# Second operand of two leaky activations read from PSUM

## The reference

```python
def _leaky(x):
    return jnp.where(x >= 0, x, LEAKY_SLOPE * x)        # LEAKY_SLOPE = 0.01
...
gp = _leaky(jnp.einsum('th,ehm->etm', x, w_gate))       # 8 experts, m = 128
up = jnp.einsum('th,ehm->etm', x, w_up)
y_all = jnp.einsum('etm,emh->eth', gp * up, w_down)
...                                                     # the two chosen experts, weighted
p = _leaky(hidden_states @ sw_gate) * (hidden_states @ sw_up) @ sw_down   # shared, 256 wide
y = y + p
```

## Time and profile before

| | us |
|---|---|
| median of 3 executions | 2302.65 |
| the three executions | 2302.65, 2306.17, 2302.55 |
| the profiled execution | 2303.26 |
| its span, first to last instruction | 2301.5 |
| shared expert, first L2270 to last L2275 | 1193.8 to 1266.7 |
| tile mixture, first L2149 to last L2154 | 1277.9 to 1366.0 |

### The profile page before, as it was taken

The page is one execution under the profiler, slowest core; times in us unless marked ns, Lnnn a source line. Parts: engine busy times, 40 slices in busy tenths (PEclk is TensorE's granted clock), DMA queues, the critical chain, the costliest instruction groups (busy, mean ns, idle before and its releaser), DMA issues. The chain is left out here.

```text
span 2301.5 us, 44687 instructions
## 1 busy us (share of the span) xinstructions
PE 2009.0 (87%) x15891; PEld 1415.9 (62%) x15891; DVE 1115.0 (48%) x3338; ACT 990.1 (43%) x2602; POOL 585.4 (25%) x972
## 2 busy tenths in 40 slices
PE   6899999887999996899967775996879999969994
PEld 3477777654777775566644454883557777736662
DVE  5388882264888824200043346106568883331112
ACT  2388881155888811111113231223668883212221
POOL 2022210076111105211124243115821111421111
PEclk9999999898999998899978985998989999979997
DMA  2185523001643121433121532741010004131113
GB/s 84 51 241 153 149 63 96 0 1 43 166 112 105 44 74 44 145 103 103 54 95 55 161 116 87 238 140 41 1 50 21 21 12 148 45 121 47 46 44 118
DMA packets 156763, 197.80 MB, mean 86 GB/s; under 512 B 15187, under 2 KB 129838, under 8 KB 156556
## 3 DMA queue, kind: packets, MB, share of 16 engines
q1 hardware_dynamic: 144940, 168.83, 24.1%
q0 software_dynamic: 11616, 26.26, 3.2%
HBM read 120.33 MB, written 88.64 MB: 91 GB/s over the span
## 5 line engine op out<-in xcount | busy, mean ns | idle before, releaser
L990 ACT ACTIVATE att_pr<-all_h,att_nmax 128x128 f32<-128x128 f32 (+3 forms) x768 | 420.8, 551 | 50.7 <-DVE att_nmax L943 50.7
L1054 PEld LDWEIGHTS att_t_ps<-all_ident,att_pr 64*128 64x128 f32 x3840 | 163.1, 139 | 104.3 <-issue 48.7
L1054 PE MATMUL att_t_ps<-all_ident,att_pr 64*128 64x64 f32 x3840 | 170.0, 223 | 10.4 <-DVE att_pt L952 10.3
L1249 PE MATMUL out_y_ps<-outw_wo,mem_qt 128*128 128x256 f32 x768 | 178.5, 386 | 0.0
L1897 PE MATMUL exp_f_h_ps<-exp_f_xs_t,cw_f_w 128*128 128x512 f32 (+1 forms) x512 | 171.9, 495 | 1.5 <-DVE exp_f_xs_t L1934 1.5
L1909 PE MATMUL exp_f_y_ps<-cw_f_w,exp_f_hid 128*128 128x256 f32 x768 | 168.4, 379 | 0.0
L952 DVE COPY att_pt<-att_t_ps 128x1024 f32<-128x1024 f32 (+2 forms) x168 | 166.5, 991 | 0.0
L1249 PEld LDWEIGHTS out_y_ps<-outw_wo,mem_qt 128*128 128x128 f32 x768 | 144.3, 193 | 24.8 <-issue 6.2
L1964 ACT ACTIVATE exp_f_hid<-exp_f_h_ps 128x512 f32<-128x512 f32 (+1 forms) x128 | 62.5, 491 | 221.0 <-PE exp_f_h_ps L1897 218.1
L1909 PEld LDWEIGHTS exp_f_y_ps<-cw_f_w,exp_f_hid 128*128 128x128 f32 x768 | 144.8, 190 | 19.5 <-issue 0.5
L943 DVE CUSTOM_DVE_ANT_0 all_h<-att_s_ps,att_bias,mem1k_nsn 128x128 f32<-128x128 f32 (+3 forms) x256 | 128.3, 548 | 35.6 <-PE att_s_ps L1037 26.7
(11 more groups left out here) (390 smaller groups left out, 3712.4 us busy)
## 6 DMA issues: line engine op xcount, KB each, us to landing
sorted_c<-all_zero SPq DMA_DIRECT2D x8, 2056.0 KB, 13.8
sorted_f<-all_zero SPq DMA_DIRECT2D x8, 2056.0 KB, 11.9
cw_f_w<-in_L_ffn_w_dram SPq DMA_DIRECT2D x16, 1024.0 KB, 8.0
cw_f_w<-in_L_ffn_W_dram SPq DMA_DIRECT2D x16, 1024.0 KB, 8.1
com_f_rows<-expert_f SPq DMA_DIRECT2D x20, 512.0 KB, 6.7
band<-rev SPq DMA_DIRECT2D x2, 4096.0 KB, 19.4
att_bias<-band SPq DMA_DIRECT2D x32, 256.0 KB, 3.0
tw_f_wab<-in_L_ffn_w_dram SPq DMA_DIRECT2D x2, 4096.0 KB, 19.7
```

The lines of the kernel that those rows point to most:

```text
L990: nc.scalar.activation(pr[u % 4][:, hh, at], sc[u % 4][:, hh, at], ACT.Exp, scale=-1.0, bias=nmax[:, b + k, q, h:h + 1], accum_out=rsum[:, ...
L1054: last = nc.tensor.transpose(t_ps[e % 2][:, half, (q + 1) * (n * hh + k) + kb, :], pr[u % 4][d, hh, at:at + P], c.ident[d, d])
L1249: nc.tensor.matmul(y_ps[b % 2][:, q, :], c.out_t[:, p, P * at:P * (at + 1)], wo[:, p, :], start=(p == 0), stop=False)
```

## The change

In both places the leaky activation's second tensor operand (`in1`) becomes the gate half of the PSUM tile, in place of the SBUF copy that ScalarE made of it. The first operand stays that copy, so ScalarE's copy, its semaphore and VectorE's waits stay as they are. No instruction is added, removed or moved, and no wait is changed.

```diff
@@ experts_by_tile, block.vector
-                        nc.vector.scalar_tensor_tensor(out=lin[t % 2][:], in0=act[t % 2][:], scalar=0.01, in1=act[t % 2][:], op0=ALU.mult,
+                        nc.vector.scalar_tensor_tensor(out=lin[t % 2][:], in0=act[t % 2][:], scalar=0.01, in1=ab_ps[t % 2][:, 0, :], op0=ALU.mult,
                                                        op1=ALU.max).then_inc(lin_ready, 1)
@@ SharedExpert.vector
-            nc.vector.scalar_tensor_tensor(out=self.lin[n][:], in0=self.act[n][:], scalar=0.01, in1=self.act[n][:], op0=ALU.mult,
+            nc.vector.scalar_tensor_tensor(out=self.lin[n][:], in0=self.act[n][:], scalar=0.01, in1=self.gu_ps[n][:, 0, :], op0=ALU.mult,
                                            op1=ALU.max).then_inc(self.lin_ready, 1)
```

## The result

| | before | after |
|---|---|---|
| median, us | 2302.65 | 2316.55 |
| lowest and highest execution | 2300.18 to 2306.96 | 2313.43 to 2321.47 |
| profiled execution, us | 2303.26 | 2321.47 |
| its span, us | 2301.5 | 2319.7 |
| first to last L2270, us | 72.1 | 85.9 |

The medians are of five executions each, taken in one comparison. The ratio is 1.0067, with a 95% interval of 1.0050 to 1.0084. The forecast was no change, with a range of 2299.5 to 2306.3 us. It was wrong: the kernel is 13.9 us slower.

What follows compares the result with a forecast made beforehand. TensorE (87% of the span) was taken to bound the tile mixture; VectorE (48%) was not the bound on average. Path terms, none there and -0.015 us in the shared expert, added 0.0 to the 2302.65 us median: 2302.7, range 2299.5 to 2306.3.

Steps and rivals of the forecast that it cites:

- Length of the instructions: Both stages: changed instructions last as long as neighbours with one PSUM operand, L2149 287 ns and L2270 421 ns.
- The dear end: Both stages: upper bound from attention's custom instruction, 348 and 479 ns, 3.4 us in all if everything were on the path.
- What the spread can give back: Shared expert: L2270's excess over its shortest, if lost to a neighbour and gone after the change, returns at most 0.14 us.
- the change part by part: Both stages: order and waits stay, only 55 instructions' operand place changes; busy time -0.08 us (L2270) and +0.20 us (L2149).
- How much of it lies on the path: Tile mixture: none; shared expert: -0.015 us, or +0.16 us at the upper bound.
- 3 instructions of 16 count: Shared expert: TensorE waited for `shx_hid` in 3 of 16 tiles, so only those lengths matter, 3 x -5 ns.
- Rival 1: TensorE, after waits on `hid`: a few ns of shift add one 10 us low-clock stretch, 4.9 us, 2307.6 us; chance 0.04.
- Rivals 2 to 4: Both stages: all PSUM start-ups exposed, 2306.1 (chance 0.04); low-clock stretch avoided, 2299.2 or 2297.8 (0.04); operand still SBUF, 2302.65 (under 0.01).
- The tile mixture: L2149's edit puts nothing on the path, as VectorE waits 0.94 us for TensorE in each tile.
- the cover that the prediction counted on: Tile mixture: VectorE's 0.94 us wait, and 0.56 us in the last tile, would absorb even 66 ns more.
- sign of error: Another granted clock in 1250 to 1290 us, a new TensorE wait on `til_c_hid`, or changed lengths in untouched stages.
- sign of being right: Both stages: windows keep the same lengths and granted clocks; L2149 near 287 ns, L2270 at 421 ns.

Runs made afterwards that it cites:

- e12: Only the shared expert's L2270 takes its second operand from PSUM, against the kernel before, in a group with late releases: ratio 1.0057.
- e2: Only the tile mixture's L2149 takes its second operand from PSUM, against the kernel before, in a group without late releases: ratio 0.9995.
- e8: Only the tile mixture's L2149 takes its second operand from PSUM, run again against the kernel before, without late releases: ratio 1.0.
- e13: Only the tile mixture's L2149 takes its second operand from PSUM, against the kernel before, in a group with late releases: ratio 1.0004.
- e17: The full change plus one small extra VectorE copy ahead of each L2270, against the kernel before, with late releases: ratio 1.0001.
- e1: Only the shared expert's L2270 takes its second operand from PSUM, against the kernel before, in a group without late releases: ratio 0.9995.
- e7: Only the shared expert's L2270 takes its second operand from PSUM, run again against the kernel before, without late releases: ratio 1.0.
- e15: The changed kernel with POOL's 32 indirect DMAs held back until the shared expert is through, against the kernel before: 2340.85 us, ratio 1.0166.
- e18: The kernel before with POOL's 32 indirect DMAs held back until the shared expert is through, against the kernel before: 2336.92 us, ratio 1.0151.
- e6: The unchanged kernel before, submitted as its own rival in a group with late releases: ratio 1.0 (0.9981 to 1.0019).

## Why the prediction was wrong, point by point

- **Length of the instructions.** Right, and a little better than taken: L2149 279 ns for 287, L2270 422 ns for 421. The dear end (348 and 479) is out. The Trainium skill, "VectorE: DVE Perf Modes", section on the TRN2 errata, would have had 62 cycles more for a PSUM source. The trace disagrees, as it did before: the medians went down by 3 and 4 ns.
- **What the spread can give back.** Here the working failed. The step is the one in "the change part by part": "its cost is the length of an instruction". The prediction saw that L2270 took 0.47 us where a POOL instruction began beside it, and closed with "no more than 0.14 us in either reading". The 0.05 us were indeed given back: no L2270 is above 422 ns now. The Trainium skill, "SBUF — State Buffer", section "Who interferes with whom", says that a VectorE instruction with two SBUF inputs contends with a GpSimd one that reads SBUF, and one with a single SBUF input does not; the trace agrees, with 468 against 422 ns at the most. But a bound on the busy time is no bound on the result: it was a bound only as long as nothing behind it depended on order. What the runs showed in its place is 13.9 us (0.57% in e12, with L2270's edit alone), which come as TensorE's idle time and slower clock, and not as VectorE's busy time.
- **How much of it lies on the path.** "3 instructions of 16 count" was read from who waited for `shx_hid`. That view shows only waits for the changed result. The thirteen others have a second way out: VectorE's later steps on the same engine, among them the positions that let POOL go. The second L2270, where the table's two groups part, isn't among the three.
- **The waits that were not read.** The waits view of the stage before showed it: L1739, L2253, L2258 and L2261 waited 16.5 us for releases of TensorE that the profile calls remote (5.3 + 6.4 + 2.8 + 2.0), long after TensorE was done. In a stage with such waits the lengths of its instructions alone don't say when things start, and it deserved a rival. None of the rivals has it.
- **Rival 1** had the sign and half of the mechanism: more time at the lower of TensorE's two levels after an idle stretch. It was put at one stretch of 10 us, 4.9 us in all, after a wait on `hid`. Measured: a wait of 11.3 us on the turned tokens first, and then 10 us at a mean clock of 0.60. Idle time brought 10.1 us and the slower clock 3.7. So the term was too small, and it hung on the wrong wait.
- **Rivals 2 to 4.** Out: the instructions got no longer, the time did not fall, and the rows name the PSUM tile.
- **The tile mixture.** Right: no cost at all (e2, e8 and e13 within 0.05%). L2149 even got 3 ns shorter, so the cover that the prediction counted on was not needed. Its 0.94 us "in each tile" was read from one row; the shortest such waits in the profile of before are 0.78 and 0.82 us.
- **What would show it.** The prediction's own sign of error, another granted clock in 1250 to 1290 us, looked at the wrong end of the stage: the new wait and the slower clock sit at 1210 to 1232. Its sign of being right, windows of both stages with the same lengths, did catch it (86.8 us for 73.0).

## What to carry to other kernels

Before calling an edit of some ns free, look in its stage for waits that end long after the instruction they wait for, and for engines that start at the same moment as the edited one; where both are there, the order of events can be a race, and the edit's price is then the price of the other outcome, here 14 us for 50 ns. Test such an edit with a small shift added to it: if the cost goes away, as in e17, it was not in the instruction itself. And compare in more than one group of runs, on more than one chip: the shared expert's edit was level with the kernel before in two groups (e1, e7) and 0.57% slower in a third (e12).

## What the hardware showed that was not expected

- Releases by TensorE reached ScalarE up to 10 us late (L1639 ended at 1210.07, the copy began at 1220.19) while POOL issued an indirect DMA of rows every 1.28 us, and this one came only 2.2 us after POOL's batch had ended. With the DMAs moved out of the way none was late in the stage (e15, e18).
- This comes in some groups of runs and not in others: the kernel before took 2300.9 to 2302.7 us in those that have it and 2289.0 in those that haven't, 0.5 to 0.6% apart. The shared expert, unchanged, took 66 to 72 us (before, e6, e13) against 56 (e2, e8).
- Which of VectorE and POOL takes longer where they meet went by how far apart they began: 0.06 us ahead, VectorE's instruction took 519 ns for 479; 0.11 us ahead, POOL's took 1.22 us for 0.98.
